# Routed rows in a decoder layer: scattered to tile order in two token groups, results written to six rows per token

## The reference

```python
shared_out = _silu_and_mul(xf @ shared_w1.T) @ shared_w2.T          # 352 shared hidden units
probs = jax.nn.softmax(xf @ gate_w.T, axis=-1)                       # 2048 tokens x 16 experts
routing_weights, selected = jax.lax.top_k(probs, 6)                  # not renormed
combine = zeros((T, E)).at[arange(T)[:, None], selected].add(routing_weights)
gate_up = jnp.einsum('th,eoh->teo', xf, w1)                          # 176 hidden units an expert
act = _silu_and_mul(gate_up)
moe_out = jnp.einsum('te,tei,ehi->th', combine, act, w2)
return moe_out + shared_out
```

## Time and profile before

| | |
|---|---|
| median of 3 runs (1446.76 to 1465.6) | 1464.87 us |
| the profiled execution, as a run | 1467.7 us |
| its span, first to last instruction | 1465.9 us |
| PE busy in the span | 1283.9 us, 88% |
| DVE, ACT, POOL busy | 59%, 48%, 43% |
| mean granted clock of PE | 0.951 |
| indirect gathers, POOL L2021 | 111, 109.8 us busy |
| indirect adds, POOL L2029 | 111, 176.0 us busy |

### The profile page before, as it was taken

The page is one execution under the profiler, slowest core; times in us unless marked ns, Lnnn a source line. Parts: engine busy times, 40 slices in busy tenths (PEclk is TensorE's granted clock), DMA queues, the critical chain, the costliest instruction groups (busy, mean ns, idle before and its releaser), DMA issues.

```text
span 1465.9 us, 28356 instructions
## 1 busy us (share of the span) xinstructions
PE 1283.9 (88%) x9022; PEld 889.7 (61%) x9022; DVE 861.9 (59%) x2469; ACT 703.6 (48%) x2991; POOL 633.6 (43%) x633
## 2 busy tenths in 40 slices
PE   5899999999987799999999998956888888888882
PEld 4688888888875566656666656744444444444441
DVE  7888888888876675656565676674223233232322
ACT  3788888888875444444444446300222222222220
POOL 3222222222111354544454544054667667666762
PEclk9899999999998999999999999965889999999996
DMA  5101101101041010010100103710444444444447
GB/s 202 30 16 38 31 16 37 30 16 24 22 152 32 1 70 1 1 70 1 70 1 1 34 19 103 188 48 19 67 68 75 68 72 75 69 71 75 77 68 197
DMA packets 64746, 82.65 MB, mean 56 GB/s; under 512 B 11520, under 2 KB 55424, under 8 KB 63840
## 3 DMA queue, kind: packets, MB, share of 16 engines
q0 software_dynamic: 21312, 30.02, 12.7%
q1 hardware_dynamic: 43296, 50.87, 11.6%
HBM read 49.00 MB, written 23.47 MB: 49 GB/s over the span
## 4 chain that ended last, share of the span: by engine, by line
PE 51%; issue 17%; POOL 11%; DVE 9%; ACT 6%; DMA 5%; SPq 0%; POOLq 0%; DVEq 0%; ACTq 0%
PE ps L573 15%; POOL xnt L2021 5%; PE ps L689 5%; PE ps L758 4%; PE ps L721 4%; DMA xnt<-xrow_d,idx 4%; PE ps L862 4%; POOL acc_d L2029 3%; ACT ea L1639 3%; PE ps L712 2%; PE ps L852 2%; PE ps L834 2%; PE ps L842 2%; PE ps L628 2%; POOL onr L2013 2%
## 5 line engine op out<-in xcount | busy, mean ns | idle before, releaser
L2029 POOL DMA_INDIRECT acc_d<-yt,idx x111 | 176.0, 1586 | 114.3 <-DVE yt L1584 83.8
L1024 PE MATMUL ps<-w,xt 128*128 x444 | 173.1, 515 | 1.7 <-ACT xt L1606 1.7
L1874 POOL TENSOR_TENSOR ea<-ea,rden 128x128 f32<-128x128 f32 (+1 forms) x128 | 62.2, 507 | 258.1 <-DVE rden L1186 258.1
L1639 ACT ACTIVATE ea<-ps,negmax 128x64 f32<-128x64 f32 (+1 forms) x512 | 164.6, 341 | 6.0 <-DVE negmax L1230 6.0
L1606 ACT ACTIVATE pt<-ps 128x512 f32<-128x512 f32 x128 | 76.8, 600 | 181.2 <-PE ps L842 122.6
L1277 DVE TENSOR_TENSOR qcs<-ps,tabb 128x512 f32<-128x512 f32 x192 | 123.6, 686 | 53.4 <-PE ps L573 53.1
L1822 ACT ACTIVATE st<-ps 128x176 f32<-128x176 f32 x111 | 35.2, 317 | 244.6 <-PE ps L1024 209.1
L1881 POOL TENSOR_TENSOR eb<-eb,rsum 128x512 f32<-128x512 f32 x64 | 66.9, 1045 | 158.2 <-DVE rsum L1321 158.2
L2021 POOL DMA_INDIRECT xnt<-xrow_d,idx x111 | 109.8, 989 | 37.5 <-issue 31.7
L1024 PEld LDWEIGHTS ps<-w,xt 128*128 128x128 f32 x444 | 79.8, 200 | 66.6 <-issue 45.1
L1584 DVE TENSOR_SCALAR yt<-ps,wt 128x256 f32<-128x256 f32 x111 | 53.7, 484 | 112.4 <-PE ps L1043 112.4
(11 more groups left out here) (208 smaller groups left out, 3415.4 us busy)
## 6 DMA issues: line engine op xcount, KB each, us to landing
raw_w<-in_rawb_dram SPq DMA_DIRECT2D x4, 2432.0 KB, 8.9
kva<-ktmp SPq DMA_DIRECT2D x64, 128.0 KB, 2.3
w<-in_rawc_dram SPq DMA_DIRECT2D x16, 320.0 KB, 5.4
raw_a<-in_wqk_dram SPq DMA_DIRECT2D x4, 768.0 KB, 5.6
x_sb<-x_dram SPq DMA_DIRECT2D x4, 512.0 KB, 6.7
raw_w<-in_wo_dram SPq DMA_DIRECT2D x1, 2048.0 KB, 11.9
acc_d<-zeros SPq DMA_DIRECT2D x4, 512.0 KB, 4.8
xrow_d<-xnt SPq DMA_DIRECT2D x4, 512.0 KB, 3.2
```

The lines of the kernel that those rows point to most:

```text
L1024: last = pe.matmul(ps[:, C_G[i % 2], 0:2 * EI].rearrange("p (m n) -> p m n", m=2), xt[:, i % 2, kt, :], w1[kt][:, :, :].rearrange("p m (e ...
L1639: last = act.activation(dst(m, h), src, ACT.Exp, bias=negmax[:, par, i:i + 1], accum_out=sums[:, par, i:i + 1])
L1874: last = pool.tensor_tensor(part, part, rden[:, par, XP * i:XP * (i + 1)].unsqueeze(2) .broadcast_to([128, XP, (QH, S)[i]]), ALU.mult)
L2029: pool.indirect_dma_start(out=acc_d[i % NACC][:, :], out_offset=bass.IndirectOffsetOnAxis(ap=idx[:, i:i + 1], axis=0), in_=yt[:, i % 3, :] ...
```

## The change

- **Two token groups.** The routing runs twice: for chunk 0 (4 sequences, at most 39 tiles) and for chunks 1 to 3 (12 sequences, at most 87 tiles), `NT` = 126. Group 0's logits, `gate`, ranks and `place` (now 34 steps in all) stand in the last units of B, group 1's behind the sixth shared unit and ahead of the tiles. The logits have the tokens as stationary matrix, 128 at a time, so they come out by token; nothing is turned.
- **Rows scattered.** There are no lists. A token's row, with its 256 features, six tile numbers, six weights and six target rows (`XROW` = 274), stays in SBUF, and POOL writes it to its six places in `xs_d` by plain indirect DMAs, one for each sequence and choice: 24 for group 0, 72 for group 1. `xs_d` has been zeroed by SP, in 16 pieces behind the key copies of A.
- **Tiles loaded in a row.** SP loads tile `i` with a plain DMA from `xs_d`; DVE picks weight and target by the tile number.
- **Results.** Group 0's tiles are stored as they are by SP (`ya_d`); POOL gathers a token's six rows by 24 indirect DMAs during group 1, and DVE sums them four times in the loop. Group 1's tiles go by one plain indirect DMA each (POOL) to six rows per token in `yb_d`, padding rows to a spare tile; SP loads them at the end, a sequence at a time, and DVE sums them. Nothing accumulates in DRAM.
- **Expert weights.** SP sorts them in DRAM (42 DMAs in A, behind the same key copies), and loads them in four plain DMAs.
- **Shared units split.** Six (chunks 0 and 1) run before the tiles, six behind them, with DVE's last sums between.

```diff
-NT = (B * S * TOPK + E * 127) // 128
-XROW = DM + E
+C_AHEAD = 2 * SH_N
+R_CHUNKS = [[0], [1, 2, 3]]
+R_SEQS = [len(ch) * CB for ch in R_CHUNKS]
+R_TILES = [(n * S * TOPK + E * 127) // 128 for n in R_SEQS]
+NA, NT = R_TILES[0], sum(R_TILES)
+XROW = DM + 3 * TOPK
+XG, YR = 6, 4
...
+            def background(n):                      # sync, behind the key copies of (g, c), n = g * NC + c
+                sp.dma_start(xs_d[128 * first:128 * last].rearrange("(t p) n -> p t n", p=128),
+                             zeros[:, :].unsqueeze(1).broadcast_to([128, last - first, XROW])).then_inc(d_init, 16)
+                for k in range(sorts * n // (NG * NC), sorts * (n + 1) // (NG * NC)):
+                    sort_weights(k)
...
+            def load_rows(i):                       # sync
+                if i == 0:
+                    sp.wait_ge(c_dn, C_AHEAD)
+                    sp.wait_ge(c_l, C_AHEAD)
+                    sp.wait_ge(r_sc[0], 16 * R_SEQS[0] * TOPK)
+                if i == NA:
+                    sp.wait_ge(r_sc[1], 16 * R_SEQS[1] * TOPK)
+                if i >= XG:
+                    sp.wait_ge(d_tx, i - XG + 1)
+                    sp.wait_ge(d_w1s, i - XG + 1)
+                sp.dma_start(xg[:, i % XG, :], xs_d[128 * i:128 * (i + 1)]).then_inc(d_xg[i % XG], 16)
...
+            for i in range(NT):
+                load_rows(i)
+                if XG - 1 <= i < NA + XG - 1:
+                    store_rows(i - (XG - 1))
...
+            for i in range(NT - YR, NT):
+                sp.wait_ge(d_sy[i % YR], uses(i))
+            sp.wait_ge(d_dn, NT)
+            for b in range(R_SEQS[1]):
+                first = 128 * YR + S * TOPK * b
+                sp.dma_start(fin[b], yb_d[first:first + S * TOPK].rearrange("(p k) d -> p (k d)", k=TOPK)).then_inc(d_fl[b], 16)
...
-            for k, (c, t) in enumerate(C_FIRST):    # tensor
+            for k, (c, t) in enumerate(C_FIRST[:C_AHEAD]):
                 c_unit(k, c, t)
-            c_list()
+            pe.wait_ge(c_y, 2)
+            r_ranks(1)
...
+            for k, (c, t) in enumerate(C_FIRST[:C_AHEAD]):    # vector
+                c_unit(k, c, t)
+            c_add(C_AHEAD - 1, 1)
+            for i in range(3):
+                gate(1, i)
+            place(1)
...
+            def six_sum(src, dst, done):
+                return dve.tensor_reduce(dst, src.rearrange("p (k d) -> p d k", k=TOPK), axis=AX.X, op=ALU.add).then_inc(done, 1)
+            A_SUMS = {NA + 24 + 16 * b: b for b in range(R_SEQS[0])}
...
+            for k, (c, t) in enumerate(C_FIRST):
+                if k >= C_AHEAD:
+                    c_unit(k, c, t)
+                    if k >= C_AHEAD + 2:
+                        last_sum(k - C_AHEAD - 2)
+            c_add(len(C_FIRST) - 1, NC - 1)
+            for b in range(SH_N * (NC - 2) - 2, R_SEQS[1]):
+                last_sum(b)
...
+            place_rows(0, 0, 8)                     # gpsimd; place_rows: one indirect DMA for each (sequence, choice)
             ln_low(2 * NC + 2)
+            place_rows(0, 8, 16)
             ln_low(3 * NC - 1)
+            place_rows(0, 16, R_SEQS[0] * TOPK)
+            place_rows(1, 0, R_SEQS[1] * TOPK)
...
+            for i in range(NA, NT):
+                spread_rows(i)
+                n = i - NA - 2
+                if 0 <= n and n % 2 == 0 and n // 2 < R_SEQS[0] * TOPK:
+                    gather_six(n // 2 // TOPK, n // 2 % TOPK)
```

More of the change, by code:

```diff
@@ L47 @@
 RB_N = RB_WO + HG * DM
-GATE_STEPS = 16
-PLACED = GATE_STEPS + 15
+EQ = 32
 EQ = 32
@@ L525, in load_down @@
-            def load_down(dst, first, rows, done):
-                for e in range(E):
-                    to = 0
-                    for tile, row, n in hidden_runs(EI * e + first, EI * e + first + rows):
-                        g, t = tile // TG, tile % TG
-                        sp.dma_start(dst[to:to + n, e, :], in_rawc[g][row:row + n, RC_T * t + 512:RC_T * (t + 1)])\
-                          .then_inc(done, 16)
-                        to += n
-            store_rows(0)
-            store_rows(1)
+            sp.wait_ge(b_it, BF + (NG - 1) * BN + len(B_PLACES[True]))
@@ L1045, in d_down @@
                   .then_inc(d_dn, 1)
[L1047 to L1052 removed]
+            pe.wait_ge(d_w1, 16 * KT)
+            pe.wait_ge(d_w2a, 16)
+            pe.wait_ge(d_w2b, 16)
             held_at = {}
@@ L1349, in b_unit @@
+                if drain and u == 0:
+                    place(0)
                 if drain and u == 2:
                     ln_stats(11)
-            steps = [0]
-            def step(ins):
-                steps[0] += 1
-                ins.then_inc(c_gs, 1)
-                dve.wait_ge(c_gs, steps[0])
-            def c_zero():
-                dve.wait_ge(b_it, BF + (NG - 1) * BN + len(B_PLACES[True]))
-                dve.memset(gone[:, :, :], 1.0).then_inc(c_z, 1)
-                dve.wait_ge(c_z, 1)
-                dve.memset(gone[:, :, 0:1], 0.0).then_inc(c_z, 1)
@@ new lines, in gate @@
+                    dve.wait_ge(r_lg[r], 1)
+                    step(r, dve.tensor_reduce(t["gmx"][:, :], logits, axis=AX.X, op=ALU.max, negate=True))
+                    step(r, dve.tensor_tensor(gl[:, :, :], logits, over_e(t["gmx"]), ALU.add))
+                    assert steps[r] == R_EXP
+                elif i == 1:
+                    dve.wait_ge(r_ge[r], 1)
+                    step(r, dve.tensor_reduce(t["gsum"][:, :], ge[:, :, :], axis=AX.X, op=ALU.add))
+                    step(r, dve.reciprocal(t["grec"][:, :], t["gsum"][:, :]))
+                    step(r, dve.tensor_tensor(gp[:, :, :], ge[:, :, :], over_e(t["grec"]), ALU.mult))
+                    for b in range(nb):
@@ L2003, in _, with place_rows @@
             ln_rstd(3 * NC - 1)
+            pool.iota(tok6[:, :, :], [[S * TOPK, R_SEQS[1]], [1, TOPK]], base=128 * YR, channel_multiplier=TOPK, **f).then_inc(r_t6, 1)
+            def place_rows(r, first, last):
+                if first == 0:
+                    pool.wait_ge(r_gs[r], R_ROWS[r])
+                    pool.wait_ge(d_init, 16 * NG * NC)
+                for n in range(first, last):
+                    b, k = n // TOPK, n % TOPK
+                    rows = chunk_rows(2 * NC + R_CHUNKS[r][b // CB])
+                    pool.indirect_dma_start(out=xs_d[:, :], out_offset=bass.IndirectOffsetOnAxis(ap=R[r]["posi"][:, b, k:k + 1], axis=0),
+                                            in_=rows[:, b % CB, :], in_offset=None).then_inc(r_sc[r], 16)
@@ new lines, in spread_rows, with gather_six @@
+            def spread_rows(i):
+                pool.wait_ge(d_y, i + 1)
+                pool.wait_ge(d_id, i - NA + 1)
+                pool.indirect_dma_start(out=yb_d[:, :], out_offset=bass.IndirectOffsetOnAxis(ap=idi[:, i % YR:i % YR + 1], axis=0),
+                                        in_=yt[:, i % YR, :], in_offset=None).then_inc(d_sy[i % YR], 16)
+            def gather_six(b, k):
+                if b == 0 and k == 0:
+                    pool.wait_ge(r_sc[1], 16 * R_SEQS[1] * TOPK)
+                    for i in range(NA - YR, NA):
+                        pool.wait_ge(d_ys[i % YR], uses(i))
+                if k == 0 and b >= 2:
+                    pool.wait_ge(d_as, b - 1)
+                pool.indirect_dma_start(out=fa[b % 2][:, DM * k:DM * (k + 1)], out_offset=None, in_=ya_d[:, :],
+                                        in_offset=bass.IndirectOffsetOnAxis(ap=ra["posi"][:, b, k:k + 1], axis=0))\
+                    .then_inc(d_ag[b % 2], 16)
```

604 lines of the change are left out of this document (299 added, 305 removed).

## The result

| | before | after |
|---|---|---|
| median | 1465.23 us (1446.76 to 1466.74) | 1491.94 us (1488.03 to 1492.78) |
| ratio, 95% interval | | 1.0207, 1.0123 to 1.0290 |
| profiled span | 1465.9 us | 1490.9 us |
| mean granted clock of PE | 0.951 | 0.936 |

The forecast was 1399. The kernel became slower, by 2.1%; the interval of 1.2 to 2.9% leaves open whether by more than 2%. The busy time by stretch says where the earlier trace rows; the columns are as there.

The account below looks back on a forecast made before the run. The prediction took POOL's queue, not PE, to bound the tile loop at 3.83 us a tile. Tiles beginning at 963, a loop of 380 and a tail of 56 summed to 1399 us; range 1372 to 1448.

Parts of the forecast that it names:

- The scatters' price: POOL's plain indirect scatter in the tile loop: taken as the gather's, 0.99 + 0.30 us; upper price 1.59 + 0.31.
- part 4: Tile loop: 126 tiles at 2.88 us make 363, with small terms 380; last tile done at 1343.
- 23 us to spare: Group 1's 72 scatters last from 962 to 1058, before tile 39 wants its rows at 1081.
- The rival that ended slower: POOL becomes the bound if a scatter costs above 2.4 us: 1467 there, 1640 at 3.5; chance 0.07.
- The pace of the loop: Tile loop: tile after tile 2.88 us apart on PE, 126 tiles in 363 us.
- The terms for the clock and late tiles: Tile loop additions: 5 us for the clock after the idle stretch, 6 for late tiles and granted clock.
- Part 1: Group 0's routing at the end of cross attention: 11 us of DVE work, partly in gaps, delays shared units 7 us.
- The bound of 11: Upper bound in us for the delay of the shared units by group 0's routing, forecast as 7.
- Part 2: Six shared units ahead of the tiles, with the logits' new form at +4 us: second chunk added at 944.
- Part 3: Group 1's routing, exposed between shared units and tiles: 19 us, so tiles begin at 963.
- Part 5: Tail after the last tile: units and adds 31.5 us, eight six-row sums 18, last store 6.5, together 56.
- The lock of descriptors: Skill rule: GpSimd's DMA descriptor writes are locked out while VectorE holds their shared ports, about 3.1 us instead of 0.62.

Follow-up runs that it names:

- e17_two_a_tile_timed: Changed kernel with group 1's scatters issued two per group 0 tile, each pair waiting for that tile's turned rows, timed in rounds: 1404.90 us, 0.9661 of the kernel before.
- e4_two_a_tile: Changed kernel with group 1's 72 scatters issued two per group 0 tile, each pair waiting for that tile's turned rows; one execution: 1400.36 us.
- e15_tree: Changed kernel with two scatters a tile and the twelve last six-row sums as additions of contiguous columns: 1394.34 us.
- set 3: Runs on one chip: changed kernel unaltered 1492.62 us, two scatters a tile 1409.01, 64-byte rows 1490.61, no group 1 scatters 1408.46; kernel before 1462.41.

## Why the prediction was wrong

The span is 92 us above the forecast: tiles begin 15 late, the loop takes 72 more, the tail 5. `e17_two_a_tile_timed` serves as the kernel without the hold-up.

- **The scatters' price (part 4) was right and its use wrong.** 72 at 1.27 us ended at 1068.6, tile 39 had its rows, no gap there. The step that failed is the overlap that was put at nothing: the 72 scatters run beside the tiles, end with "23 us to spare", and so cost nothing. In one set they cost 84 us (1492.62 against 1408.46 without them). The rival that ended slower had the right place (POOL's queue against the loop) and the wrong mechanism: POOL wasn't slow, PE was. The loop, from the routing's end (977.9, DVE's last step) to the last scaled result (1429.7), took 452 us instead of 380; with two a tile 365 (976.5 to 1341.3).
- **The pace of the loop was right.** 126 x 2.88 with next to nothing on top: 365 where I had 380. The terms for the clock and late tiles (11 us) were not needed: the loop with pairs runs at a granted clock of 1.00 from 987 to 1078. The low clock and the late tiles of the earlier trace rows stood beside a loop that POOL bounded; that this was their cause is not shown apart.
- **Part 1, 7 us late: 16** (first hidden product 921.93, against 906.19). The mechanism was the one named, `obl` behind the routing, but I let DVE's gaps take part of it. PE stood idle for 7.86 us until 912.39, just behind the end of `obl`, which DVE made here (last line: PE's next matmul):

```profile
904.06 0.21 DVE L1483 COPY r_ggt<-ps 128x64 f32<-128x64 f32 x1
...
904.80 1.66 DVE L1486 TENSOR_TENSOR r_gl<-r_geq,thr 128x64 f32<-128x64 f32 x1
...
911.67 0.15 DVE L1521 TENSOR_SCALAR r_texp<-r_tsum 128x1 int32<-128x1 f32 x1
911.86 0.42 DVE L1365 TENSOR_TENSOR obl<-ps,obh 128x256 fp32r<-128x256 f32 x1
...
912.39 0.77 PE L633 MATMUL ps<-xnh,wch 128*128 128x512 f32 x1 [7.86 <-issue]
```

  All 7.8 us of `place(0)` fall on the path, since it stands ahead of the last `obl` in the queue. One step took 1.66 us instead of 0.22, beside POOL's subtraction, as in the earlier trace rows. The bound of 11 was too low as well. In the other 8 us lies an earlier wait of PE for `obl` of 2.80 us (at most 0.88 in the kernel before); the rest isn't traced.
- **Part 2, 944: 959.9.** 8.7 of the 16 us are part 1's. Another 4.7 lie between the first and the sixth hidden product: the logits took 8.15 us instead of 6.8, at a granted clock of 0.77 from 935 to 945; `e4_two_a_tile`, at 0.95 there, made them in 5.4. The rest is `c_add`, which waited 3.9 us for a signal of PE that group 0's scatters held up (1.8 in `e17_two_a_tile_timed`).
- **Part 3, 19 us: right,** 18 (959.9 to 977.9). So the exposed routing can be summed from the earlier trace rows and its element counts, the comparisons at 1.36 us each instead of 1.22.
- **Part 5, 56 us: 61.** The six-row sum was mis-sized:

```profile
L1650 DVE TENSOR_REDUCE xt<-w x6: 2731/2731/2826, 1458.1 to 1475.1; 128x256 f32<-128x1536 f32 x6
```

  2.73 us instead of 1.8. I took the slope of contiguous reductions, 1.06 ns an element; with neighbours 256 elements apart it is 1.7. Small groups alone don't make a sum dearer, at least down to 16, since this contiguous one by 16 fits the 1.06:

```profile
910.61 0.55 DVE L1517 TENSOR_REDUCE xnt<-r_eq 128x24 f32<-128x384 f32 x1
```

  The contiguous additions of `e15_tree` make the sum and its add in 0.95 and three times 0.42 us. The Trainium skill, "SBUF — State Buffer", section "Door 1: The DMA port swizzle", says that an access pays for each new 16-byte line, so that float32 can be strided by 4 at most for free; these rows agree, and I should have weighed it. Twelve sums were 11 us dearer than forecast, of which the loads and a store of 3.3 us instead of 6.4 gave some back.
- **The lock of descriptors didn't show.** The scatters on POOL took 0.96 us in the median and 1.45 at most, beside all that DVE did. The Trainium skill, "SBUF — State Buffer", section "SBUF: two separate sides", says of the engines' ports to SBUF that only the pair shared by VectorE and GpSimd causes contention and that PE never waits there. PE was held up all the same while POOL issued (1492.62 against 1408.46 us in set 3). These runs don't show that it happened at a port of SBUF, so they neither confirm nor refute the rule; it can't be taken to say that POOL's DMAs leave PE alone.

In sum the forecast of 1399 is close to what the change does with its scatters in pairs and no hold-up (`e4_two_a_tile` 1400, `e17_two_a_tile_timed` 1405). That is partly luck, by errors that cancel: start 13 later, loop 15 shorter, tail 5 longer. It was no forecast of this kernel, because it asked of a moved queue only whether it would finish in time.

## To carry over

A long row of indirect DMAs on GpSimd isn't free because it finishes in time: tie it to the consumer's progress, one or two for each step of the loop. That cost nothing that could be measured here, and it brought 1492 down to 1409 where PE was held up. All of this was seen in recorded executions. Put the steps of a routing behind the last operation that TensorE still waits for, not ahead of it, and sum rows as contiguous additions. And when chips or sets can differ, run the unchanged kernel beside the edits: one set alone would have taught that small rows cure.

## What the hardware showed that I had not expected

- PE's signals came up to 40 us late by the record while POOL issued indirect DMAs 1.27 us apart, at about 2.6 to 3.1 us a matmul. ACT's and DVE's came in 0.01 us.
- It happened in three sets of experiments and in the first measurement, and not in two sets, one of them on a chip that had shown it before. One and the same program took 1490.6 us in one set and 1405.3 in another.
- Rows of 64, 512 and 1096 bytes did it alike; plain DMAs of POOL, 0.53 us apart, did not.
- Where PE was held up, the traces had also lost semaphore changes (10287 against 13619 for one kernel), under indirect DMAs and not under plain ones.
